# First weights in four loads and transposed by VectorE, in a gated convolution pair on one core

## The chip, the core and the metric

One NeuronCore of a Trainium2 chip. The time is the device time of one execution in microseconds (us). The engines are TensorE (PE), VectorE (DVE), ScalarE (ACT), GpSimd (POOL) and SyncE (SP); SP, ACT and POOL also issue DMAs, each on a queue of its own.

## The reference, cut to what matters

```python
def qconv_cg(x, w, theta):                 # 64 channels, the first 16 are the "base"
    yp = conv3x3(x[:, :16], w[:, :16])
    yr = conv3x3(x[:, 16:], w[:, 16:])
    d = sigmoid(2.0 * (yp - theta))
    return yp + d * yr

h = relu(bn(qconv_cg(x, w_a, theta_a), gamma_a, beta_a, mean_a, var_a))
h = bn(qconv_cg(h, w_b, theta_b), gamma_b, beta_b, mean_b, var_b)
return relu(x + h)                         # x: (16, 64, 56, 56), w: (64, 64, 3, 3), float32
```

## The kernel before

The 64 channels are four groups of 16. Each group has 32 partitions, since a partition holds one of two row parities of a channel, and each group of 32 rows of TensorE's array works alone, so four products with 32 rows run beside each other. Group 0 gives yp, groups 1 to 3 add up to yr. Values are split into a high and a low part (`x_hi`, `x_lo`, `w_hi`, `w_lo`), and three kinds of product are summed: high x with high w, high x with low w, low x with high w. With six taps (two slot offsets `c`, three columns `dx`) that makes 18 units for a visit of a group to a block: units 0 to 5 need `w_hi`, the second half of it from unit 3 on; units 6 to 11 need `w_lo`; units 12 to 17 need `x_lo`. TensorE's program is written out in steps, one unit of each active group for a step (L554). Group 2 begins its first visit at step 6 and group 3 at step 12; until then a product that nobody reads (L580) stands in their place. At step 24 a small transpose of the parameters stands (L572), from which VectorE works out the batch norms' constants. The first block takes 7 slots of the first image. In all there are 108 blocks, of the first and the second convolution in turn.

The start is what the change is about:

- SP loads all of `w_a` as it lies in memory, output channels on 64 partitions (L402, 144 KB), then chunks of x (L371), then `w_b` in four loads by group (L411, 36 KB each), input channels to be. ACT issues two of the x loads.
- VectorE writes zeros (L756 to L767), then copies w_a with the parities side by side into `w_pad` (L769, L771); ScalarE does two rows of it (L652).
- TensorE multiplies zeros from `h_lo`, which GpSimd has set (L437), two small products and seven large ones (L500), then does 12 transposes of `w_pad` into PSUM (L494), then one small product.
- ScalarE makes `w_hi` from PSUM (L640), VectorE the high part of the first x chunk (L839), `w_lo` (L776) and the `x_lo` parts (L835).
- GpSimd makes the identity matrix (L438, L440), issues ten loads of parameters (L445), then writes zeros into the padding of `h_hi` and `h_lo` and goes on to the weights of the edges.
- The second weights already go the other way: the four loads (L411), eight transposes by VectorE (L790), ScalarE's high part (L645), VectorE's low part (L797).

Engines run their own programs in order and meet at semaphores.

Of the kernel before, what the change touches and what calls it, by code (L numbers as in the profile page):

```python
# [5 lines left out]
ALU = mybir.AluOpType  # L6
# [4 lines left out]
P = 128  # L11
# [22 lines left out]
SMALL, WARM, BRIDGE = 2, 7, 1  # L34
# [6 lines left out]
def gated_conv_pair_kernel(nc, x, w_a, theta_a, gamma_a, beta_a, mean_a, var_a,  # L41
# [119 lines left out]
    with ExitStack() as ctx:  # L161
# [21 lines left out]
        NAT, PAD = C * TAPS * TAPS, (TAPS + 1) * TAPS * C * 2  # L183
        HALF_NAT = GR * TAPS * TAPS


        AT_B = NAT + PAD
        AT_T = AT_B + 5 * HALF_NAT
        early = sb("early", [P, AT_T + 2 * TAPS * P])
        w_nat_a = early[0:C, 0:NAT]  # L190

        w_pad = early[0:C, NAT:AT_B].rearrange("o (r b i q) -> o r b i q", r=TAPS + 1, b=TAPS, q=2)
        zeros_b = early[:, AT_B:AT_T].rearrange("p (z n) -> p z n", n=HALF_NAT)[:, 0:5:2]
        w_nat_b = early[:, AT_B:AT_T].rearrange("p (z n) -> p z n", n=HALF_NAT)[:, 1:5:2]

        w_t = early[:, AT_T:AT_T + 2 * TAPS * P].rearrange("p (t m) -> p t m", m=P)
        e_hi = sb("e_hi", [P, 2, EDGE_COLS], F32R)
        e_lo = sb("e_lo", [P, 2, EDGE_COLS], F32R)
        x_edge = early[:, 0:EDGE * W]
# [28 lines left out]
        wpad_ready = sem("wpad_ready")  # L228
        wpad_odd_ready = sem("wpad_odd_ready")
        wzeros_ready = sem("wzeros_ready")  # L230
        wbt_ready = sem("wbt_ready")
        zeros_ready = sem("zeros_ready")
        warm_done = sem("warm_done")
        wt_ready = sem("wt_ready")
# [107 lines left out]
        def natural_a(rows):  # L342

            return w_nat_a.rearrange("o (i a b) -> o a b i", a=TAPS, b=TAPS)[:, rows]
# [41 lines left out]
        def _(sp):  # L386
# [15 lines left out]
            sp.dma_start(w_nat_a, w_a.rearrange("o i a b -> o (i a b)")).then_inc(w_landed[0], 16)  # L402
# [16 lines left out]

            sp.wait_ge(wt_ready, 2)  # L420
# [14 lines left out]
        def _(pool):  # L435
            for lo, hi in ((0, P), (P, BANK)):
                nc.gpsimd.memset(h_lo[:, lo:hi].bitcast(F32), 0.0).then_inc(zeros_ready, 1)  # L437
# [9 lines left out]
            for n, t in enumerate((h_hi, h_lo)):  # L447
                if t is h_lo:
                    pool.wait_ge(zeros_ready, 2)
                    pool.wait_ge(warm_done, 1)  # L450
                nc.gpsimd.memset(t[:, 0:1].bitcast(F32), 0.0)
                nc.gpsimd.memset(t[:, 1::PITCH].bitcast(F32), 0.0).then_inc(hpads_zero, 2)
# [33 lines left out]
        def _(pe):  # L486
            def weights(c, bank):

                pe.wait_ge(wpad_ready, 3 + c)
                pe.wait_ge(wpad_odd_ready, 1 + c)  # L490
                for dx in range(TAPS):
                    to = psum[:, bank, dx * P:(dx + 1) * P].rearrange("p (c q) -> p q c", q=2)
                    for mq in range(2):
                        last = pe.transpose(to[:, mq], w_pad[:, 2 * c - mq + 1, dx].rearrange("o i q -> o (i q)"),  # L494
                                            ident[:])
                last.then_inc(wt_ready, 1)
# [72 lines left out]
            for step in sorted(steps):  # L569
                if step == 24:  # L570
                    pe.wait_ge(prmdup_ready, 2)
                    pe.transpose(psum[:, 7, 0:10], prm_dup[:].rearrange("n c q -> n (c q)"),  # L572
                                 ident[0:10, 0:10]).then_inc(prmT_ready, 1)
                for g in (2, 3):
                    if step < OFFSET[g]:

                        if step == 0:
                            pe.wait_ge(xhi0_ready, 1)
                            pe.wait_ge(whi_ready, 1)
                        pe.matmul(psum[:, g - 1, 0:SPARE], w_hi[0][g * ROWS:(g + 1) * ROWS, 0],  # L580
                                  x_hi[g * ROWS:(g + 1) * ROWS, 0, 1:1 + SPARE], start=True, stop=True)
                for g, visit, u in steps[step]:
                    b = visited(g, visit)
                    kind, n = blk = order[b]
                    if u == 0 and g == bank_groups(b)[0]:
                        if kind == "a":
                            if n == 0:
                                pe.wait_ge(xhi0_ready, 1)
                                pe.wait_ge(whi_ready, 1)
# [32 lines left out]
                    if g == 0 and u == 0 and b == 1:  # L622
                        pe.wait_ge(wlo_ready, 2)
                    if g == 0 and u == 0 and b == 2:
                        pe.wait_ge(rvar_ready, 1)
                    if u == 0 and b == WARM_BANK and g == bank_groups(b)[0]:
                        pe.wait_ge(warm_done, 1)
# [9 lines left out]
        def _(act):  # L637
            def weights_hi(c, bank):
                act.wait_ge(wt_ready, c + 1)
                nc.scalar.activation(w_hi[0][:, c * TAPS:(c + 1) * TAPS].rearrange("p t m -> p (t m)"),  # L640
# [330 lines left out]
```

## Time and profile before

| | us |
|---|---|
| runs | 436.45, 434.79, 434.56 |
| median | 434.79 |
| profiled execution, its own time | 434.86 |
| its span, first to last instruction | 433.0 |
| TensorE busy in the span | 425.9 |

The span is what the profile shows; the 1.9 us between it and the execution's own time lie around it.

### The profile page before, as it was taken

Reading aid. Unit: us, or ns where it says so; the run is one execution under the profiler, and the core shown is the slowest. Engines: PE = TensorE matmul, PEld = TensorE weight load, DVE = VectorE, ACT = ScalarE, POOL = GpSimd, SP = SyncE. Lnnn points to the kernel's source line nnn. Section 1 sums busy time; section 2 is a strip of 40 time slices with the busy share of each in tenths; the row PEclk is TensorE's granted clock in tenths of the full one; section 3 lists DMA queues with packets and bytes.
Section 4 is the critical chain, followed back from the end, with each engine's and each line's share of the span. In section 5 each row is a group of like instructions: output and inputs, shape, how many; then the busy total and the mean of one; then the engine's idle time right before and its main releaser. Section 6 shows DMA issues by size and latency. Waiting matters only on the chain.

```text
span 433.0 us, 17317 instructions
## 1 busy us (share of the span) xinstructions
PE 425.9 (98%) x7817; PEld 423.0 (98%) x7817; DVE 246.6 (57%) x420; ACT 198.8 (46%) x337; POOL 30.2 (7%) x83
## 2 busy tenths in 40 slices
PE   9999999999999999999999999999999999999994
PEld 7999999999999999999999999999999999999993
DVE  6767644753764663574375385366357367436535
ACT  5765444534544553453453453354345355434322
POOL 6041000000000100000000000011000000000001
PEclk9999999999999999999999999999999999999998
DMA  8435116241515110420624161161623322012044
GB/s 170 83 78 99 27 27 124 50 98 30 122 28 101 25 28 3 100 51 2 125 58 81 37 122 30 27 122 25 122 49 61 67 49 45 8 27 49 8 93 94
DMA packets 119802, 27.57 MB, mean 64 GB/s; under 512 B 119408, under 2 KB 119664, under 8 KB 119728
## 3 DMA queue, kind: packets, MB, share of 16 engines
q1 hardware_dynamic: 117296, 25.99, 29.4%
q8 instruction: 62, 1.02, 1.0%
q10 hardware_dynamic: 2112, 0.46, 0.5%
q14 instruction: 12, 0.10, 0.1%
q0 software_dynamic: 320, 0.00, 0.0%
HBM read 13.60 MB, written 12.85 MB: 61 GB/s over the span
## 4 chain that ended last, share of the span: by engine, by line
PE 97%; DVE 1%; issue 0%; ACT 0%; POOL 0%; DVEq 0%; POOLq 0%
PE acc L554 96%; PE acc L500 1%; DVE mix L858 0%; DVE rows_out L906 0%; PE acc L494 0%; PE acc L580 0%; ACT mix L697 0%; DVE rows_out L948 0%; DVE rows_out L903 0%; POOL h_lo L437 0%; ACT rows_out L719 0%; DVEq L857 0%; POOLq L960 0%
## 5 line engine op out<-in xcount | busy, mean ns | idle before, releaser
L554 PE MATMUL acc<-x_lo,w_hi 32*128 32x456 f32 (+1 forms) x1392 | 248.4, 358 | 0.0
L554 PE MATMUL acc<-x_hi,w_lo 32*128 32x456 f32 (+1 forms) x1392 | 248.2, 358 | 0.0
L554 PE MATMUL acc<-x_hi,w_hi 32*128 32x456 f32 (+1 forms) x1392 | 247.7, 358 | 0.0
L554 PE MATMUL acc<-h_hi,w_lo 32*128 32x512 f32 x1152 | 241.4, 390 | 0.0
L554 PE MATMUL acc<-h_lo,w_hi 32*128 32x512 f32 x1152 | 241.0, 390 | 0.0
L554 PE MATMUL acc<-h_hi,w_hi 32*128 32x512 f32 x1152 | 240.7, 389 | 0.0
L554 PEld LDWEIGHTS acc<-x_hi,w_hi 32*128 32x128 f32 x1392 | 208.5, 183 | 0.4
L554 PEld LDWEIGHTS acc<-x_hi,w_lo 32*128 32x128 f32 x1392 | 208.6, 183 | 0.2
L554 PEld LDWEIGHTS acc<-x_lo,w_hi 32*128 32x128 f32 x1392 | 208.5, 183 | 0.0
L554 PEld LDWEIGHTS acc<-h_hi,w_hi 32*128 32x128 f32 x1152 | 181.3, 183 | 0.1
L554 PEld LDWEIGHTS acc<-h_lo,w_hi 32*128 32x128 f32 x1152 | 181.3, 184 | 0.1
L554 PEld LDWEIGHTS acc<-h_hi,w_lo 32*128 32x128 f32 x1152 | 181.0, 184 | 0.2
L697 ACT ACTIVATE mix<-acc,gate_bias 128x448 f32<-128x448 f32 (+2 forms) x108 | 69.5, 644 | 176.4 <-PE acc L554 176.3
L858 DVE TENSOR_TENSOR mix<-mix,acc 128x448 f32<-128x448 f32 (+2 forms) x108 | 68.4, 634 | 105.2 <-PE acc L554 104.9
L885 DVE SCALAR_TENSOR_TENSOR rows_out<-acc,inv,x 128x504 f32<-128x504 f32 x46 | 34.0, 739 | 53.1 <-ACT mix L697 53.1
L719 ACT ACTIVATE rows_out<-rows_out,shift 128x504 f32<-128x504 f32 (+1 forms) x49 | 35.0, 715 | 33.5 <-DVE rows_out L906 32.8
L702 ACT ACTIVATE z<-acc,shift,inv 128x448 f32<-128x448 f32 (+1 forms) x58 | 40.8, 704 | 0.0
L893 DVE SCALAR_TENSOR_TENSOR mix<-mix,inv,z 128x448 f32<-128x448 f32 (+1 forms) x58 | 38.9, 671 | 2.0
L715 ACT ACTIVATE h_hi<-mix 128x448 fp32r<-128x448 f32 (+1 forms) x58 | 32.2, 564 | 13.8 <-DVE mix L893 13.4
L835 DVE TENSOR_TENSOR x_lo<-x,x_hi 128x448 fp32r<-128x448 f32 (+3 forms) x52 | 33.5, 678 | 7.1 <-ACT x_hi L665 7.0
L906 DVE SCALAR_TENSOR_TENSOR rows_out<-mix,inv,rows_out 128x504 f32<-128x504 f32 (+1 forms) x48 | 35.7, 744 | 1.7
L921 DVE SCALAR_TENSOR_TENSOR h_lo<-mix,h_hi 128x448 fp32r<-128x448 f32 (+2 forms) x64 | 33.1, 567 | 0.1
(85 smaller groups left out, 157.3 us busy)
## 6 DMA issues: line engine op xcount, KB each, us to landing
out_dram<-rows_out SPq DMA_DIRECT2D x95, 126.0 KB, 2.6
x<-in_x_dram SPq DMA_DIRECT2D x28, 392.0 KB, 5.3
early<-in_x_dram SPq DMA_DIRECT2D x4, 112.0 KB, 4.0
out_dram<-rows_out SPq DMA_DIRECT2D x3, 112.0 KB, 2.8
x<-in_x_dram SPq DMA_DIRECT2D x3, 98.0 KB, 3.8
x<-in_x_dram SPq DMA_DIRECT2D x1, 294.0 KB, 4.2
x<-in_x_dram SPq DMA_DIRECT2D x1, 280.0 KB, 4.9
x<-in_x_dram SPq DMA_DIRECT2D x1, 196.0 KB, 4.1
```

The lines of the kernel that those rows point to most:

```text
L500: return pe.matmul(psum[:, WARM_BANK, 0:n], h_lo[:, 0:P], h_lo[:, 0:n], start=True, stop=True)
L554: return pe.matmul(sums(bank, blk), w[g * ROWS:(g + 1) * ROWS, tap], moving(blk, part, c, dx, g), start=(u == 0 and (alone or g == bank_gr ...
L697: nc.scalar.activation(mix_rows(b), yp_rows(b), ACT.Sigmoid, scale=ALPHA, bias=gate_bias[:, k:k + 1]).then_inc(gate_ready, 1)
L702: nc.scalar.activation(z_of(n).rearrange("p (s w) -> p s w", w=W), yp_rows(b), ACT.Identity, scale=inv[:, 0:1], bias=shift[:, 0:1]).then_i ...
L715: nc.scalar.activation(in_middle(h_hi, n), as_block(mixed(b), n), ACT.Relu).then_inc(hhi_ready, 1)
L719: nc.scalar.activation(out_of(m), out_of(m), ACT.Relu, bias=shift[:, 1:2]).then_inc(out_ready, 1)
L835: nc.vector.tensor_tensor(split_chunk(x_lo, n), x_chunk(n), split_chunk(x_hi, n).bitcast(F32), ALU.subtract).then_inc(xlo_ready, 1)
L858: nc.vector.tensor_tensor(mix_rows(b), mix_rows(b), yr_rows(b), ALU.mult).then_inc(gated_ready, 1)
L885: nc.vector.scalar_tensor_tensor(to, yp_rows(b), inv[:, 1:2], was, ALU.mult, ALU.add).then_inc(zb_ready, 1)
L893: nc.vector.scalar_tensor_tensor(mixed(b), mixed(b), inv[:, 0:1], z_of(n), ALU.mult, ALU.add).then_inc(summed_ready, 1)
L906: nc.vector.scalar_tensor_tensor(out_of(m), mixed(b), inv[:, 1:2], out_of(m), ALU.mult, ALU.add).then_inc(summed_ready, 1)
L921: nc.vector.scalar_tensor_tensor(part[0], part[1], 0.0, part[2], ALU.max, ALU.subtract).then_inc(hlo_ready, 2 // images)
```

## The change

- `w_a` comes in four loads by group, of 36 KB each, in the form that `w_b` has: group 0 from SP, group 1 from ACT ahead of its x loads, groups 2 and 3 from GpSimd ahead of all its other work. They land in `natural`, beside columns of zeros that VectorE sets after the first x padding.
- VectorE does the transposes, eight by 32x32 blocks into `w_t` in SBUF. `w_pad`, its copies and TensorE's 12 transposes are gone.
- ScalarE makes the high part of the first x chunk, then `w_hi` of tap 0 alone (`wtap_ready`), then the rest of the first half, then the second half. The first unit waits for tap 0 only, unit 1 for the first half.
- VectorE makes both halves of `w_lo` from SBUF before its `x_lo` parts.
- TensorE's products on zeros read a constant in both operands, ten large and four small, one after the other up to the first unit; no wait ahead of them, and none for them afterwards.
- `w_b`'s loads wait until w_a is transposed, since they go to the same place. `x_edge` has its own space.

```diff
-SMALL, WARM, BRIDGE = 2, 7, 1
+WARM, BRIDGE = 10, 4
...
+        x_edge = sb("x_edge", [P, EDGE * W])
...
+        natural = sb("natural", [P, 5, HALF_NAT])
+
+        w_t = sb("w_t", [P, 2 * TAPS, P])
...
+        def load_w(eng, w, g, done):
+
+            eng.dma_start(natural[g * ROWS:(g + 1) * ROWS, 1:4:2],
+                          w.rearrange("(h o) (g i) a b -> g o h (i a b)", h=2, g=GROUPS)[g]).then_inc(done, 16)
...
-            sp.dma_start(w_nat_a, w_a.rearrange("o i a b -> o (i a b)")).then_inc(w_landed[0], 16)
+            load_w(sp, w_a, 0, w_landed[0])
...
+
+            sp.wait_ge(wt_ready[0], 2)
             for g in range(GROUPS):
-                sp.dma_start(w_nat_b[g * ROWS:(g + 1) * ROWS],
-                             w_b.rearrange("(h o) (g i) a b -> g o h (i a b)", h=2, g=GROUPS)[g]
-                             ).then_inc(w_landed[1], 16)
+                load_w(sp, w_b, g, w_landed[1])
...
-            for lo, hi in ((0, P), (P, BANK)):
-                nc.gpsimd.memset(h_lo[:, lo:hi].bitcast(F32), 0.0).then_inc(zeros_ready, 1)
+            for g in (2, 3):
+                load_w(pool, w_a, g, w_landed_pool)
...
+            def zeros(n):
+
+                return nc.const_aps.tensor(0.0, (P, n), F32).bitcast(F32R)
...
-                return pe.matmul(psum[:, WARM_BANK, 0:n], h_lo[:, 0:P], h_lo[:, 0:n], start=True, stop=True)
-
-            pe.wait_ge(zeros_ready, 1)
-            for n in range(SMALL):
-                zeros_product(P)
-            pe.wait_ge(zeros_ready, 2)
+                return pe.matmul(psum[:, WARM_BANK, 0:n], zeros(P), zeros(n), start=True, stop=True)
+
             for n in range(WARM):
                 zeros_product(BANK)
-            pe.wait_ge(ident_ready, 2)
-            for c in range(2):
-                weights(c, 6 + c)
             for n in range(BRIDGE):
-                mm = zeros_product(P)
-            mm.then_inc(warm_done, 1)
+                zeros_product(P)
...
-                                pe.wait_ge(whi_ready, 1)
+                                pe.wait_ge(wtap_ready, 1)
...
+                    if b == 0 and g == 1 and u == 1:
+                        pe.wait_ge(whi_ready, 1)
...
+            load_w(nc.scalar, w_a, 1, w_landed[0])
             act.wait_ge(xpads_zero, 1)
             load_x(nc.scalar, 0, 0, SHORT + 1, x_first[0], (1,))
             load_x(nc.scalar, 0, SHORT + 1, 2 * SHORT + 1, x_second, (1,))
-            weights_odd()
-            for c in range(2):
-                weights_hi(c, 6 + c)
             act.wait_ge(xcols_zero, 1)
+            act.wait_ge(x_first[0], 32)
+            nc.scalar.activation(split_chunk(x_hi, 0), x_chunk(0), ACT.Copy).then_inc(xhi0_ready, 1)
+
+            act.wait_ge(wt_ready[0], 1)
+            weights_hi(0, slice(0, 1)).then_inc(wtap_ready, 1)
+            weights_hi(0, slice(1, TAPS)).then_inc(whi_ready, 1)
+            act.wait_ge(wt_ready[0], 2)
+            weights_hi(0, slice(TAPS, 2 * TAPS)).then_inc(whi_ready, 1)
...
             zero_x_pads(0, 1)
+            nc.vector.memset(natural[:, 0:5:2], 0.0).then_inc(wzeros_ready, 1)
             zero_x_pads(1, X_IMGS)
...
+            def transposed(k, c):
+
+                for mq in range(2):
+                    for h in range(2):
+                        rows = filter_rows(natural[:, 2 * h:2 * h + 3].rearrange("p z n -> p (z n)"),
+                                           2 * c - mq + 1, slice(0, TAPS))
+                        to = w_t[:, c * TAPS:(c + 1) * TAPS].rearrange("p t (o q) -> p t o q", q=2)
+                        last = nc.vector.transpose(to[:, :, h * ROWS:(h + 1) * ROWS, mq],
+                                                   rows.rearrange("p i q b -> p b i q"))
+                last.then_inc(wt_ready[k], 1)
...
+            def first_weights():
+                dve.wait_ge(w_landed[0], 32)
+                dve.wait_ge(w_landed_pool, 32)
                 dve.wait_ge(wzeros_ready, 1)
                 for c in range(2):
+                    transposed(0, c)
+                for c in range(2):
+                    dve.wait_ge(whi_ready, c + 1)
+                    weights_lo(0, c)
...
-            dve.wait_ge(x_first[0], 32)
-            nc.vector.tensor_copy(split_chunk(x_hi, 0), x_chunk(0)).then_inc(xhi0_ready, 1)
-            for c in range(2):
-                weights_lo(c, 6 + c)
+            first_weights()
             for n in range(SOON):
                 split_lo(n)
```

## Rows read from the trace of the kernel before

**Rows 1.** The page: busy time, DMA queue, share of the chain by engine.
```profile
PE 425.9 (98%) x7817; PEld 423.0 (98%) x7817; DVE 246.6 (57%) x420; ACT 198.8 (46%) x337; POOL 30.2 (7%) x83
...
q0 software_dynamic: 320, 0.00, 0.0%
...
PE 97%; DVE 1%; issue 0%; ACT 0%; POOL 0%; DVEq 0%; POOLq 0%
```

**Rows 2.** The chain that ended last, in order of time: start, us, what.
```profile
0.99 3.78 PE acc L500 x9
4.78 1.22 PE acc L494 x12
...
6.28 0.55 PE acc L580 x2
...
8.83 414.39 PE acc L554 x6868
```

**Rows 3.** PE's timeline: start, us, instruction, count.
```profile
1.48 1.59 PE L500 MATMUL acc<-h_lo 128*128 128x512 f32 x3
...
2.01 1.48 PE L500 MATMUL acc<-h_lo 128*128 128x512 f32 x3
...
3.72 1.05 PE L500 MATMUL acc<-h_lo 128*128 128x512 f32 x2
...
7.15 0.36 PE L554 MATMUL acc<-x_hi,w_hi 32*128 32x398 f32 x2
...
8.79 0.37 PE L554 MATMUL acc<-x_lo,w_hi 32*128 32x398 f32 x2
...
10.98 0.17 PE L572 MATMUL acc<-ident,prm_dup 10*128 10x10 f32 x1
```

**Rows 4.** One stretch of PE: us, busy (instructions), granted clock, DMA share, GB/s.
```profile
2.50:5.00 2.50, 2.50 (x9) 1.00 0.99 212
```

**Rows 5.** VectorE's timeline, in brackets idle time before and its releaser.
```profile
0.83 0.62 DVE L756 MEMSET x<- 128x112 f32 x2 [0.83 <-PEq L960]
...
3.77 0.76 DVE L769 COPY early<-early 64x384 f32<-64x384 f32 x1 [1.02 <-DMA early<-in_L_conv_w_a_dram]
...
6.17 1.02 DVE L776 TENSOR_TENSOR w_lo<-acc,w_hi 128x384 fp32r<-128x384 f32 x2 [0.31 <-ACT w_hi L640]
...
9.58 0.29 DVE L846 COPY prm_dup<-prm_rows 10x64 f32<-10x64 f32 x2 [0.38 <-DMA prm_rows<-in_L_conv_var_b_dram]
...
17.87 1.92 DVE L790 STREAM_TRANSPOSE early<-early 128x96 f32<-128x96 f32 x8
```

**Rows 6.** ScalarE's timeline.
```profile
9.85 0.20 ACT L678 ACTIVATE probe<-probe 128x1 f32<-128x1 f32 x1
...
21.34 0.94 ACT L645 ACTIVATE w_hi<-early 128x384 fp32r<-128x384 f32 x2
```

**Rows 7.** DMA issues that touch 1.3 to 2.0: KB each, us to landing.
```profile
early<-in_L_conv_w_a_dram SPq DMA_DIRECT2D x1, 144.0 KB, 3.0
x<-in_x_dram ACTq DMA_DIRECT2D x1, 112.0 KB, 3.1
x<-in_x_dram SPq DMA_DIRECT2D x1, 98.0 KB, 3.9
```

**Rows 8.** The loads of w_b (L411): ns min/median/max, and landing.
```profile
L411 SPq DMA_DIRECT2D early<-in_L_conv_w_b_dram x4: 427/430/1691, 7.5 to 10.2; - x4
...
DMA to landing us min/median/max: 2.1/2.7/3.8
```

**Rows 9.** GpSimd's ten loads of parameters (L445), landing.
```profile
DMA to landing us min/median/max: 2.5/2.9/3.3
```

**Rows 10.** GpSimd's timeline.
```profile
0.73 0.56 POOL L437 MEMSET h_lo<- 128x128 f32 x2 [0.29 <-POOLq L960]
...
2.12 0.65 POOL L445 DMA_DIRECT2D prm_rows<-in_L_conv_theta_a_dram  x1 [0.28 <-issue]
...
4.20 0.49 POOL L445 DMA_DIRECT2D prm_rows<-in_L_conv_var_a_dram  x1
```

More of the change, by code:

```diff
@@ L227, in gated_conv_pair_kernel @@
         ident_ready = sem("ident_ready")
-        wpad_ready = sem("wpad_ready")
-        wpad_odd_ready = sem("wpad_odd_ready")
         wzeros_ready = sem("wzeros_ready")
[L231 to L234, printed above, removed]
+        wt_ready = [sem(f"wt_ready{c}") for c in "ab"]
+        w_landed_pool = sem("w_landed_pool")
+        wtap_ready = sem("wtap_ready")
         whi_ready = sem("whi_ready")
@@ L446, in _ @@
                                ).then_inc(prm_landed, 16)
[L447 to L450, printed above, removed]
+            for t in (h_hi, h_lo):
                 nc.gpsimd.memset(t[:, 0:1].bitcast(F32), 0.0)
@@ L570, in _ @@
                 if step == 24:
+                    pe.wait_ge(ident_ready, 2)
                     pe.wait_ge(prmdup_ready, 2)
@@ L588, in _ @@
                                 pe.wait_ge(xhi0_ready, 1)
-                                pe.wait_ge(whi_ready, 1)
+                                pe.wait_ge(wtap_ready, 1)
                             else:
@@ L637, in _, with weights_hi @@
         def _(act):
[L638 to L641 removed]
+            def weights_hi(k, taps):
+                return nc.scalar.activation(w_hi[k][:, taps], w_t[:, taps], ACT.Copy)
             def second_weights_hi(c):
[L644 to L652 removed]
+                act.wait_ge(wt_ready[1], 2)
+                weights_hi(1, slice(c * TAPS, (c + 1) * TAPS)).then_inc(whi_ready, 1)
             def split_hi(n):
@@ L764, in _ @@
             nc.vector.memset(probe[:], 0.0).then_inc(probe_zero, 1)
-            for q in range(2):
-                nc.vector.memset(w_pad[:, TAPS * q, :, :, q], 0.0).then_inc(wpad_ready, 1)
-            nc.vector.memset(zeros_b, 0.0).then_inc(wzeros_ready, 1)
-            dve.wait_ge(w_landed[0], 16)
-            nc.vector.tensor_copy(w_pad[:, 1], natural_a(slice(0, 2)).rearrange("o a b i -> o b i a")
-                                  ).then_inc(wpad_ready, 1)
-            nc.vector.tensor_copy(w_pad[:, 2:4, :, :, 0], natural_a(slice(1, 3))).then_inc(wpad_ready, 1)
@@ L773, in weights_lo @@
-            def weights_lo(c, bank):
-                dve.wait_ge(whi_ready, c + 1)
-                part = w_hi[0][:, c * TAPS:(c + 1) * TAPS].rearrange("p t m -> p (t m)")
-                nc.vector.tensor_tensor(w_lo[0][:, c * TAPS:(c + 1) * TAPS].rearrange("p t m -> p (t m)"),
-                                        psum[:, bank, 0:TAPS * P], part.bitcast(F32),
-                                        ALU.subtract).then_inc(wlo_ready, 1)
+            def transposed(k, c):
[7 more added lines that the diff above has]
+                last.then_inc(wt_ready[k], 1)
@@ new lines, in weights_lo @@
+            def weights_lo(k, c):
+                taps = slice(c * TAPS, (c + 1) * TAPS)
+                nc.vector.tensor_tensor(w_lo[k][:, taps], w_t[:, taps], w_hi[k][:, taps].bitcast(F32),
+                                        ALU.subtract).then_inc(wlo_ready, 1)
+            def first_weights():
+                dve.wait_ge(w_landed[0], 32)
+                dve.wait_ge(w_landed_pool, 32)
+                dve.wait_ge(wzeros_ready, 1)
+                for c in range(2):
+                    transposed(0, c)
+                for c in range(2):
+                    dve.wait_ge(whi_ready, c + 1)
+                    weights_lo(0, c)
@@ L780, in second_weights @@
             def second_weights():
                 dve.wait_ge(w_landed[1], 16 * GROUPS)
-                dve.wait_ge(wzeros_ready, 1)
                 for c in range(2):
-                    for mq in range(2):
-                        for h in range(2):
-                            at = AT_B + 2 * h * HALF_NAT
-                            rows = filter_rows(early[:, at:at + 3 * HALF_NAT], 2 * c - mq + 1, slice(0, TAPS))
-                            to = w_t[:, c * TAPS:(c + 1) * TAPS].rearrange("p t (o q) -> p t o q", q=2)
-                            last = nc.vector.transpose(to[:, :, h * ROWS:(h + 1) * ROWS, mq],
-                                                       rows.rearrange("p i q b -> p b i q"))
-                    last.then_inc(wbt_ready, 2)
+                    transposed(1, c)
@@ L794, in second_weights_lo @@
             def second_weights_lo(c):
                 dve.wait_ge(whi_ready, 3 + c)
-                taps = slice(c * TAPS, (c + 1) * TAPS)
-                nc.vector.tensor_tensor(w_lo[1][:, taps], w_t[:, taps], w_hi[1][:, taps].bitcast(F32),
-                                        ALU.subtract).then_inc(wlo_ready, 1)
+                weights_lo(1, c)
             chain = [0]
```

34 lines of the change are left out of this document (removed).

## The prediction, made before the changed kernel ran

> **What bounds the kernel now.** I read the page's totals first: TensorE (PE) is busy for 425.9 of 433.0 us and carries 97% of the chain that ended last [rows 1]. So nothing that another engine does is worth anything, unless it moves the moment at which PE's real work begins, stops PE later, or changes PE's speed. Second, the chain in order of time shows where that moment is [rows 2]: PE runs products on zeros from 0.99, the twelve transposes of the first weights from 4.78, and the first product on x at 6.28; the last row shown is 414.39 us of products from 8.83 in one piece, without a gap. The change touches nothing behind the second visit. The question is only whether the products after 6.28 come earlier or later.
>
> Third, the timeline of PE fixes the reference points [rows 3]. Four row groups share the array, so a "step" is four products; steps follow one another every 0.18 us: step 3, the first that needs the second half of w_hi, has its unit at 7.15, 0.87 after the first product at 6.28, and step 12, the first with x_lo, at 8.79, nine steps and 1.64 us later. The products on zeros start every 0.43 us (2.01 to 3.72 is four of them, 1.71 us) for 512 columns, so 1.2 GHz, the lower of the two levels. A step of 398 columns in 0.18 us is 2.4 GHz. The rise lies between 3.72 and 7.15; the granted-clock column shows 1.00 there too [rows 4], so it doesn't locate the rise, and I go by the spacing.
>
> **The change part by part.** Call W the moment at which all of w_a has landed.
>
> Before, W is 3.77 [rows 5], and behind it come VectorE's and ScalarE's copies, the transposes on PE, and w_hi from PSUM [rows 2, 5]: unit 3 is at W + 3.38.
>
> After, behind W: eight transposes on VectorE, of the same tile shape as those of the second weights, 1.92 us for eight [rows 5]; four are through after 3 x 0.24 + 0.32 = 1.04 (0.24 is 1.92 / 8, 0.32 is about the duration of one, since two overlap). Then ScalarE copies tap 0 alone, 128 elements: between a copy of one element, 0.20, and one of 384, 0.52 (two overlap in 0.94) [rows 6], I take 0.3. So the first unit can go at W + 1.04 + 0.03 + 0.3 + 0.03 = W + 1.4. The second half of w_hi needs all eight transposes and a 384-element copy: W + 1.92 + 0.03 + 0.52 + 0.03 = W + 2.50 for unit 3. Counted back by the 0.55 us of three steps, the start that matters is W + 1.95, and unit 3 decides, not unit 0. The later dependencies hold. The two subtractions for w_lo (0.51 each on VectorE, [rows 5]) end at W + 2.44 and about W + 3.0, and are wanted at steps 6 and 9, W + 3.05 and W + 3.6. The low part of the first x chunk ends at W + 3.6 and is wanted at step 12, W + 4.15. ScalarE's high part of the second chunk ends 0.5 after its weights, W + 3.0, wanted at step 6, W + 3.05: just in time. Break-even with before is thus W = 7.15 - 2.50 = 4.65.
>
> Now W itself. The four loads are 36 KB each. The SP and ScalarE ones start at about 0.74; SP's single 144 KB load took 3.0 us to land, and the same 36 KB form for w_b 2.1 to 3.8 [rows 7, 8]: they land at 3.8 or before, unless the x loads crowd them. The other two are issued by GpSimd, one after the other, and the second of these sets W. The trace shows GpSimd issuing only ten rows of 0.2 KB: 0.65 us for the first, 0.48 for another, 2.5 to 3.3 us from issue to landing [rows 9, 10]. GpSimd's body starts at 0.73, where the h_lo memset stands now; the second load is issued at 0.73 + 0.65 = 1.38. With the longest landing, 3.3, since a load of 36 KB must share the DMA engines with x, W = 4.7. In front of its first DMA GpSimd also stood idle for 0.28 without a releaser [rows 10]; if that is the price of a first DMA, W = 5.0. I take 4.8. Bounds: the shortest landing gives 1.38 + 2.5 = 3.9. Upwards, a row of prm is 32 packets (320 for ten, [rows 1]), and a weight load has 64 runs each way; if GpSimd's time grew with packets to four times 0.48, 1.9 us each, W = 0.73 + 0.28 + 1.9 + 1.9 + 2.4 (landing behind the end of the issue) = 7.2. I stay near the rows, because that end rests on a count of packets alone, and no row shows an issue of GpSimd's over 0.65.
>
> The Trainium skill ("DMA: Bandwidth & Descriptors", section on the anatomy of one DMA on the GpSimd path) says that many descriptors can be emitted before their cost shows, and fits 2.0 us plus bytes over 436 GB/s. By that, an estimate, a 36 KB load would land 2.1 us after its issue, W would be set by the other queues at about 3.8, and the early rival below would be the result. Even 0.2 KB took 2.5 to 3.3 here [rows 9], so I don't follow its figure.
>
> Moved with it: x's first chunk. ScalarE issues a weight load first (0.43, the shortest of w_b's, [rows 8]), so its x load starts near 1.2, and took 3.1 to land; SP's, behind the like issue, starts near 1.2 too and took 3.9 [rows 7]: x is there by 5.1. ScalarE now makes its high part (448 elements, at most 0.6), ending at 5.7; the weights are wanted from it at W + 1.07 = 5.9. So this is covered by the wait for W; were W early, each 0.1 us by which x is late would cost 0.1 at unit 0, and nothing at unit 3 until it is 0.9.
>
> PE's own queue: its zero products need no memset, so they start at about 0.82 instead of 0.99. A small one lies between 0.11 (a quarter of 0.43) and 0.25 (two took from 0.99 to 1.48, [rows 2, 3]); I take 0.15. Ten large and four small end their issue at 0.82 + 4.3 + 0.6 = 5.7. That is a floor: PE can't take the first real product before, 0.6 ahead of 6.28. With W = 4.8 the first unit is at 6.2, so PE idles some 0.5 us, less if the small ones are dear.
>
> Prm rows: GpSimd loses two memsets (0.56) and gains two loads (1.13), so the last row lands at 9.58 + 0.57 = 10.2, and its VectorE copies (0.29) end at 10.5; PE wants them at step 24, 10.98 before [rows 3, 5, 10]. Slack shrinks from 1.1 to about 0.6 with PE's own shift, and it is kept if the loads are dearer, because PE's start then moves by as much. VectorE's memsets, the reordered one of the zero columns too, end long ahead of W. w_b's loads wait for the first transposes, over at W + 1.95 = 6.75; they took 2.7 to land and are wanted at 17.87 [rows 5, 8], so even a queue at SP a few us long hides in that. x_edge on its own space removes a wait that had long been met.
>
> **Sum.** Unit 3 at 4.8 + 2.50 = 7.30 against 7.15: +0.15 us. The profiled execution took 434.86 us for its span of 433.0, and the median of the three runs is 434.79, so I forecast 435.0 us: no measurable change. One half percent is 2.2 us, about what a measurement of this kernel can tell from no change (its own three runs spread over 1.9). With the landing between 2.9 and 3.6 and the idle 0.28 counted or not, the likeliest case's own range is 434.5 to 435.6.
>
> **The rivals.**
> - Early: GpSimd's loads land in 2.5 us, W is 3.9, and PE's queue of zero products becomes the limit: -0.6 us, 434.3. For it: the early loads have little ahead of them. Against: x crowds the DMA engines from 2.5 to 5.0, at a share of 0.99 [rows 4]. Chance 0.13.
> - Slower by GpSimd's queue: its two issues cost more than 0.48 to 0.65. The place is W; the price is what both cost more, 1 to 1. It decides from 4.65 on, and passes 2.2 us only when W passes 6.9, so near its bound of 7.2 (+2.55, 437.4). One way to it is VectorE: its memsets run from 0.83 to about 2.3, beside the issues. The first prm row took 0.65, the one at 4.20, beside VectorE's copy of 3.77 to 4.53, 0.49 [rows 5, 10]; so I price this at 0.16 each, and 1.0 for both if they waited until 2.3. Chance 0.18, of which 0.04 is over 2.2 us; typical 436.0.
> - Slower by the clock: PE idles behind its zero products, then meets the first steps at 1.2 GHz. A step of 398 columns then takes 0.33 us, not 0.18, so each us at the lower level costs 0.45 us. In the trace the level had risen at most 6.2 us after PE's first product (0.99 to 7.15). If the idle stretch made it start afresh, 6.2 x 0.45 = 2.8 us, 437.8; half of that if it carries over in part, 436.4. For it: before has no such stretch between the last zero product and the first real one. Against: it is short beside 4.9 us of products. Chance 0.07, half of it over 2.2 us.
> - The forecast: chance 0.62.
>
> **Range and chances.** Range 434.2 to 436.4: it takes in the early rival and most of the GpSimd one, and leaves out what lies behind W = 6.2 and the worse half of the clock one. Faster by over 0.5% would need 2.2 us, and the floor of PE's queue allows 0.6: 0.01. Slower: 0.04 + 0.03, rounded up for what I may have missed: 0.07. Same: 0.92.
>
> **What would show it.** In the profile after: two GpSimd DMA issues of 0.5 to 0.7 from 0.73; VectorE's first transpose at 4.8, released by a GpSimd load; tap 0 on ScalarE at 5.9; the first product on x near 6.2, and unit 3 near 7.3; steps of 0.18 from there; the 10-element transpose near 11.1 with no idle ahead of it. The prediction is wrong if the first transpose starts after 6.8, if steps of 0.33 stand behind the first unit, or if PE idles ahead of the small transpose.

## The result

The changed kernel took 436.95 us (median of 22 runs, 436.27 to 437.51). The kernel before, run 22 times beside it, took 436.44 us, and not the 434.79 of its first three runs. The ratio is 1.0029, 95% interval 1.0019 to 1.004: 0.3% slower, less than the 0.5% that this work takes as a difference, but clear of noise. The forecast of 435.0, range 434.2 to 436.4, missed it. Five executions among all that follow took 468.79 to 1090.04 us (three of before, two of e9, its profiled one among them); they are disturbed, and no count of clusters holds them.

The medians hide that both kernels fall into two clusters. Of 21 runs of before, 7 took 434.5 to 434.8 and 14 took 436.4 to 437.0. Of 22 runs of after, 11 took 436.3 to 436.9 and 11 took 437.0 to 437.5; ten of the latter have a mean granted clock of 0.990 to 0.992, all others 0.994 or more. Lower cluster against lower cluster after lost 1.8 us (0.4%), upper against upper 0.6. There are thus two questions: what the 1.8 us are, and what makes the clusters.

The profile of after is of the lower cluster: its own time is 436.57 us, its span 434.7, against 434.86 and 433.0. Its page, totals and shares of the chain, beside [rows 1]:

```profile
PE 426.2 (98%) x7809; PEld 424.0 (98%) x7809; DVE 246.1 (57%) x423; ACT 197.9 (46%) x337; POOL 30.8 (7%) x83
...
PE 95%; POOL 1%; DVE 1%; DMA 1%; issue 1%; ACT 0%; POOLq 0%; DVEq 0%
```

TensorE is as busy as before (426.2 for 425.9). The extra time is not work but waiting, and GpSimd and a DMA have come into the chain. The chain in order of time, beside [rows 2]:

```profile
1.34 1.26 POOL natural L341 x2
...
3.46 4.34 POOL prm_rows L433 x9
7.80 4.18 DMA prm_rows<-in_L_conv_var_b_dram
...
12.00 0.30 DVE prm_dup L812 x2
...
12.43 0.20 PE acc L543
12.63 412.22 PE acc L524 x6826
```

What the end goes back to is no longer the first product on x, but the parameter rows that the small transpose of step 24 wants. It stands at 12.43 where [rows 3] have 10.98.

TensorE's timeline, beside [rows 3]:

```profile
0.78 5.19 PE L478 MATMUL acc<-const-float32-0.0 128*128 128x512 f32 x14 [0.78 <-PEq L926]
7.15 0.52 PE L551 MATMUL acc<-x_hi,w_hi 32*128 32x398 f32 x2 [1.18 <-ACT w_hi L609]
...
8.01 0.36 PE L524 MATMUL acc<-x_hi,w_hi 32*128 32x398 f32 x2
...
12.43 0.20 PE L543 MATMUL acc<-ident,prm_dup 10*128 10x10 f32 x1 [0.43 <-DVE prm_dup L812]
```

The first product on x is at 7.15, 0.87 later than at 6.28, behind 1.18 us of idle time. Unit 3 is at 8.01, 0.86 behind 7.15 before: the delay comes from the first product, not from unit 3. Without another wait step 24 would stand at 10.98 + 0.87 = 11.85. It stands 0.58 later. Behind the stall the products of that step start with it at 12.44 and the next ones 0.29 later, where steps otherwise follow after 0.18:

```profile
12.44 0.45 PE L524 MATMUL acc<-x_hi,w_hi 32*128 32x398 f32 x1
...
12.73 0.33 PE L524 MATMUL acc<-x_hi,w_hi 32*128 32x398 f32 x1
```

That is another 0.11, in all 0.87 + 0.58 + 0.11 = 1.56. ScalarE's fourth gate activation, the first one that waits for TensorE, is 1.57 later (21.86 for 20.29), and the span is 1.7 longer; the last 0.1 isn't located.

ScalarE's timeline of the start, and VectorE's, beside [rows 5, 6]:

```profile
4.94 1.28 ACT L634 ACT_TABLE_LOAD   x1 [4.94 <-DMA x<-in_x_dram]
6.23 0.58 ACT L634 ACTIVATE x_hi<-x 128x448 fp32r<-128x448 f32 x1
6.72 1.01 ACT L609 ACTIVATE w_hi<-w_t 128x128 fp32r<-128x128 f32 x3
```

```profile
5.20 1.86 DVE L741 STREAM_TRANSPOSE w_t<-natural 128x96 f32<-128x96 f32 x8 [2.84 <-issue]
7.35 1.03 DVE L747 TENSOR_TENSOR w_lo<-w_t,w_hi 128x384 fp32r<-128x384 f32 x2 [0.28 <-ACT w_hi L609]
...
12.00 0.29 DVE L812 COPY prm_dup<-prm_rows 10x64 f32<-10x64 f32 x2 [1.66 <-DMA prm_rows<-in_L_conv_var_b_dram]
```

x landed at 4.94. ScalarE then loads its table for 1.28 us, and only then makes the high part and tap 0. GpSimd's timeline, beside [rows 10]:

```profile
1.34 1.26 POOL L341 DMA_DIRECT2D natural<-in_L_conv_w_a_dram  x2 [0.89 <-POOLq L926]
...
3.46 0.52 POOL L433 DMA_DIRECT2D prm_rows<-in_L_conv_theta_a_dram  x1 [0.24 <-issue]
...
7.80 0.48 POOL L433 DMA_DIRECT2D prm_rows<-in_L_conv_var_b_dram  x1
```

Its first DMA starts at 1.34, not at 0.73. The landings (DMA issues that touch 1.3 to 2.0, and 2.0 to 2.7) are 2.3 us for the first weight load and 2.7 as the median of both, so 3.1 for the second: about 2.05 + 3.1 = 5.15, and VectorE goes at 5.20.

```profile
natural<-in_L_conv_w_a_dram POOLq DMA_DIRECT2D x1, 36.0 KB, 2.3
...
natural<-in_L_conv_w_a_dram POOLq DMA_DIRECT2D x2, 36.0 KB, 2.7
```

### The profile page after: what moved, and what is told of

Read it like the earlier page. It is cut to its first block, busy times and chain, and to the rows that moved or that the text cites. A ratio compares the mean times of both kernels' runs of the same rounds, so it can differ in the third digit from the quotient of the medians.

```text
span 434.7 us, 17302 instructions
## 1 busy us (share of the span) xinstructions
PE 426.2 (98%) x7809; PEld 424.0 (98%) x7809; DVE 246.1 (57%) x423; ACT 197.9 (46%) x337; POOL 30.8 (7%) x83
## 4 chain that ended last, share of the span: by engine, by line
PE 95%; POOL 1%; DVE 1%; DMA 1%; issue 1%; ACT 0%; POOLq 0%; DVEq 0%
PE acc L524 95%; POOL prm_rows L433 1%; DMA prm_rows<-in_L_conv_var_b_dram 1%; DVE mix L824 0%; DVE rows_out L872 0%; POOL natural L341 0%; ACT mix L664 0%; DVE rows_out L914 0%; DVE prm_dup L812 0%; DVE rows_out L869 0%; POOL ident L428 0%; PE acc L543 0%; POOL ident L426 0%; POOLq L428 0%; ACT rows_out L686 0%
## 5 line engine op out<-in xcount | busy, mean ns | idle before, releaser
L524 PE MATMUL acc<-x_lo,w_hi 32*128 32x456 f32 (+1 forms) x1392 | 252.2, 358 | 0.0
L524 PE MATMUL acc<-x_hi,w_lo 32*128 32x456 f32 (+1 forms) x1392 | 251.8, 358 | 0.0
L524 PE MATMUL acc<-x_hi,w_hi 32*128 32x456 f32 (+1 forms) x1392 | 251.6, 357 | 0.0
L524 PE MATMUL acc<-h_hi,w_lo 32*128 32x512 f32 x1152 | 245.0, 390 | 0.0
L524 PE MATMUL acc<-h_lo,w_hi 32*128 32x512 f32 x1152 | 244.5, 389 | 0.0
L524 PE MATMUL acc<-h_hi,w_hi 32*128 32x512 f32 x1152 | 244.4, 389 | 0.0
L524 PEld LDWEIGHTS acc<-x_lo,w_hi 32*128 32x128 f32 x1392 | 212.7, 183 | 0.0
L524 PEld LDWEIGHTS acc<-x_hi,w_hi 32*128 32x128 f32 x1392 | 212.5, 183 | 0.1
L524 PEld LDWEIGHTS acc<-x_hi,w_lo 32*128 32x128 f32 x1392 | 212.6, 183 | 0.0
L524 PEld LDWEIGHTS acc<-h_hi,w_hi 32*128 32x128 f32 x1152 | 184.4, 183 | 0.0
```

The source lines that it names most:

```text
L524: return pe.matmul(sums(bank, blk), w[g * ROWS:(g + 1) * ROWS, tap], moving(blk, part, c, dx, g), start=(u == 0 and (alone or g == bank_gr ...
```

## The experiments

Times are medians; "before" is the kernel before, timed beside each set. Clusters are given as counts, because a median between two clusters says little. The three waits are taken first, the clock second. Each kernel computes the whole function; e6 also transposes zeros that nobody reads.

| run | us | ratio to before, 95% | clusters |
|---|---|---|---|
| e1 before again | 434.87 | 0.9988 (0.997 to 1.0007) | 7 at 434.5 to 434.9, 5 at 436.4 to 436.8 |
| e2 table early | 436.58 | 1.0020 (1.0006 to 1.0033) | 12 at 436.5 to 436.9 |
| e3 no GpSimd loads | 437.28 | 1.0033 (1.0014 to 1.0053) | 3 at 435.6 to 435.7, 9 at 437.1 to 438.9 |
| e4 both | 434.79 | 0.9978 (0.9965 to 0.9992) | 12 at 434.6 to 435.0 |
| e5 fewer zeros | 434.87 | 0.9990 (0.9973 to 1.0008) | 9 at 434.6 to 435.0, 3 at 436.0 to 436.6 |
| e6 transposes instead | 434.72 | 0.9974 (0.9958 to 0.9990) | 12 at 434.6 to 435.0 |
| e7 rows by ScalarE | 437.67 | 1.0052 (1.0030 to 1.0075) | 2 at 436.0 to 436.4, 6 at 437.6 to 437.9, 1 at 439.1 |
| e8 high part on VectorE | 434.78 | 0.9979 (0.9963 to 0.9994) | 12 at 434.6 to 434.9 |
| e9 before with the constant | 434.88 | 0.9990 (0.9974 to 1.0007) | 9 at 434.5 to 435.0, 1 at 436.7 |
| e10 third chunk split | 434.53 | 0.9975 (0.9961 to 0.9990) | 12 at 434.1 to 434.9 |
| e11 rows by SP | 435.59 | 1.0008 (0.9992 to 1.0024) | 8 at 435.3 to 435.8, 4 at 436.7 to 436.9 |
| e12 before once more | 436.61 | | 1, upper |
| e13 split, shorter zeros | 434.50 | 0.9990 (0.9974 to 1.0006) | 9 at 434.3 to 435.0, 3 at 435.8 to 436.4 |
| e14 after, longer zeros | 436.45 | 1.0026 (1.0012 to 1.0040) | 12 at 436.2 to 436.7 |

**e1, the kernel before again.** No edit.

> The kernel before, unchanged, against itself. Its 22 times lie in two clusters, 434.5 to 434.8 and 436.4 to 437.0 us. If the clusters come from TensorE's clock rising at a different moment of the start, a run of the upper cluster shows steps of 0.33 us instead of 0.18 behind the first product at 6.28, about 4 us of them (1.9 / 0.45). If they come from a wait, the steps stay at 0.18 and a gap of 1.9 us stands somewhere. Ratio 1.000 either way.

The two clusters came back, 7 to 5. In the five sets in which before was timed, 76 of its runs lie at 435.5 or below and 62 at 435.8 to 437.0. Its profile was of the lower cluster, so it didn't decide; e12's does. e1's profile shows a mean granted clock of 0.945 at 434.82 us, a usual time, which no run explains, so the mean clock alone doesn't tell a run's cluster.

**e2, the table load ahead of the wait.**

```diff
+            act.wait_ge(probe_zero, 1)
+            nc.scalar.activation(probe[:, 2:3], probe[:, 3:4], ACT.Copy)
             act.wait_ge(xcols_zero, 1)
             act.wait_ge(x_first[0], 32)
```

> The kernel after, with one activation of a single element ahead of ScalarE's wait for x, so that the table load of 1.28 us no longer hangs on that wait. Theory (the parameter rows at step 24 decide, the late first product is covered by them): the first product moves from 7.15 to about 6.65, step 24 stays at 12.4, the span stays at 434.7. Rival (the late first product is the loss): the span falls by the same 0.5 us to 434.2.

The lower cluster gained nothing: 436.58, span 434.6. The chain still goes through the rows, with the small transpose at 12.32 (12.43 in after):

```profile
7.80 4.06 DMA prm_rows<-in_L_conv_var_b_dram
...
12.32 0.20 PE acc L543
12.52 412.21 PE acc L524 x6817
```

So the late first product was covered by the late rows. The start of TensorE's products shows what the table load had hidden:

```profile
6.79 0.53 PE L551 MATMUL acc<-x_hi,w_hi 32*128 32x398 f32 x2 [0.92 <-ACT w_hi L609]
...
7.48 0.35 PE L524 MATMUL acc<-x_hi,w_hi 32*128 32x398 f32 x2
...
7.80 0.45 PE L524 MATMUL acc<-x_hi,w_hi 32*128 32x398 f32 x2
```

The first product is at 6.79 for 7.15, and unit 3 at 7.80 stands 0.32 behind unit 2, not 0.18: here unit 3 waits for the second half of w_hi, as the prediction had it. Its VectorE began to transpose at 5.32, and 5.32 + 2.50 = 7.82. In after the second half of w_hi would have let unit 3 go at about 7.76, so of the 0.86 by which it is late there some 0.6 is W and 0.25 the table load.

Something was gained in the upper cluster: none of e2's 12 runs is above 436.9, where after has 11 of 22 at 437.0 or more. TensorE stands idle for 0.92 us here, for 1.18 in after. One of e2's runs has a mean clock of 0.991 all the same, at 436.56.

Why the table load waits in after is read from the traces and not from the compiled program: with two waits ahead of the first activation it began with the landing of x (4.94); in before, with one wait there, it ran at 2.45, ahead of the landing at 3.77 that its activation waited for. So it seems that of two waits one is hung on the table load.

**e3, w_a's loads by SP and ScalarE alone,** the table load as in after.

```diff
             load_w(sp, w_a, 0, w_landed[0])
+            load_w(sp, w_a, 2, w_landed[0])
...
-            for g in (2, 3):
-                load_w(pool, w_a, g, w_landed_pool)
...
             load_w(nc.scalar, w_a, 1, w_landed[0])
+            load_w(nc.scalar, w_a, 3, w_landed[0])
```

> The kernel after, with w_a's groups 2 and 3 issued by SP and ScalarE instead of GpSimd, the table load still behind the wait for x. Theory (parameter rows decide): the last parameter row lands near 9.3 instead of 11.98, no stall at step 24; the first product is at 7.3 to 7.5, since x is issued 0.4 us later and the table load still follows it; step 24 at 12.1, span 434.2 to 434.5. Rival (what decides is W, the landing of w_a behind GpSimd): W falls from 5.2 to about 3.5 and the first product with it, by 1.0 us or more, span 433.5.

Three runs lie at 435.6 to 435.7, 0.8 below after's lower cluster. The other nine are above 437.0. The profile is one of those. The rows were there by 10.26. W fell to 3.36, yet the first product stayed at 7.16, held by the table load, so the rival fell. TensorE's stretches (length, busy and count, granted clock, DMA share, GB/s) show something new:

```profile
0.00:4.50 4.50, 3.72 (x9) 3.04 (x10) 2.48 (x14) 0.00 (x0) 3.46 (x12) 1.00 0.44 95
4.50:7.90 3.40, 1.67 (x21) 1.50 (x23) 1.26 (x6) 2.95 (x6) 3.25 (x10) 1.00 1.13 223
7.90:11.30 3.40, 3.40 (x48) 3.40 (x44) 2.64 (x8) 2.58 (x5) 0.00 (x0) 0.51 1.20 202
11.30:14.70 3.40, 3.40 (x82) 3.40 (x79) 0.72 (x5) 0.47 (x2) 0.00 (x0) 0.99 0.97 199
```

The products on zeros end early, TensorE idles 1.74 us, and then, although it works without a pause from 7.16 on, the granted clock is 0.51 from 7.9 to 11.3, the level of 1.2 GHz. 48 products fit there, 82 into the next stretch of the same length. That is the clock rival of the prediction. Six of the nine have the mean clock that one such fall gives, 0.990 to 0.992; the two longest, 438.5 and 438.9, have 0.996, and what made them longer stays open.

**e4, both edits.**

> Both edits: loads of w_a by SP and ScalarE, table load ahead of the wait for x. Theory (two waits in a row, neither worth anything alone): x's high part ends at 5.8, tap 0 at 6.2, first product 6.25, unit 3 near 7.1, no stall at step 24, span 433.0 or like before. Rival (the transposes on VectorE are slow in themselves, or TensorE's idle stretch costs clock): the span stays at 434 or above although both waits are gone.

434.79, in one narrow cluster, 1.8 below after and level with before's lower cluster. First product at 6.12, no stall at step 24. The two edits give back the whole of the lower cluster's loss: the table alone gives 0 (e2), the loads alone 0.8 (e3), both 1.8. TensorE still stands idle for 0.64 us ahead of its first product on x here, and no run lies in an upper cluster. Its chain now begins with x:

```profile
1.68 3.43 DMA x<-in_x_dram
...
5.20 0.58 ACT x_hi L635
5.78 0.21 ACT w_hi L607
...
6.12 0.53 PE acc L549 x2
```

**e7 and e11, GpSimd's loads by themselves.** To price W without the rows, five of the ten rows go to another queue, the table load is early, GpSimd keeps its weight loads.

```diff
-            for n, v in enumerate(rows):
+            for n, v in enumerate(rows[:5]):
...
+            for n, v in enumerate([theta_b, gamma_b, beta_b, mean_b, var_b]):
+                nc.scalar.dma_start(...)   # e7, behind its x loads; e11: sp.dma_start, behind image 0
```

> The kernel after with the table load early (as e2) and five of the ten parameter rows issued by ScalarE behind its x loads; GpSimd keeps its two loads of w_a. It isolates the loads by GpSimd: W stays at 5.2, the rows are there by 10. Theory (in after the parameter rows are worth the stall of 0.6 at step 24 and all that follows it, W is worth about 0.6 by itself): unit 3 at W + 2.5 = 7.7, no stall, span 433.5, time 435.3. Rival (W alone gives the loss): 434.6 span as in e2.

e7 missed its aim. ScalarE's five issues pushed its table load to 5.41, the first product came at 7.72, and the forecast of 435.3 was wrong by 0.7 to 1.1 even in its lower cluster.

```profile
5.41 1.28 ACT L637 ACT_TABLE_LOAD   x1 [5.41 <-issue]
6.71 0.20 ACT L637 ACTIVATE probe<-probe 128x1 f32<-128x1 f32 x1
6.81 0.56 ACT L640 ACTIVATE x_hi<-x 128x448 fp32r<-128x448 f32 x1
```

It does show that without the wait for rows a late first product costs its own length: it is 1.44 late, and the span, 434.4, is 1.4 above before's.

> The kernel after with the table load early and five of the ten parameter rows issued by SP behind the loads of the first image; GpSimd keeps its two loads of w_a and ScalarE has no more to issue than in after. W stays at 5.2. Theory (W by itself costs about 0.6): first product at 6.7, unit 3 at W + 2.5 = 7.7, rows there by 10, span 433.5, time 435.4. Rival (W hurts less than that): 433.0.

e11 puts the rows on SP. The first product is at 6.73 and eight runs lie at 435.3 to 435.8 (forecast 435.4), so W at 5.2 costs 0.7 by itself against e4, and the rows on GpSimd cost another 1.1 against e2. Four runs are at 436.7 to 436.9; the profile, with a clock of 0.51 from 7.0 to 10.4 behind 1.73 us of idling, is one of them. Two of the four have a mean clock of 0.991 like it, the other two 0.994, so these may have another cause.

**e12, before once more.** No edit.

> The kernel before once more, one profile. If it falls into the upper cluster (one in two), the theory of the clock says: the products on zeros run at 0.43 us, and behind the first product on x steps of 0.33 us stand for some 4 us. If it falls into the lower, it is the profile of before again.

It fell into the upper cluster, 436.61, span 434.8. Its timeline of TensorE against [rows 2, 3]:

```profile
0.99 3.78 PE L500 MATMUL acc<-h_lo 128*128 128x128 f32 x9 [0.99 <-POOL h_lo L437]
4.70 1.54 PE L494 MATMUL acc<-ident,early 64*128 64x64 f32 x12
6.17 0.47 PE L500 MATMUL acc<-h_lo 128*128 128x128 f32 x1
...
6.58 0.70 PE L554 MATMUL acc<-x_hi,w_hi 32*128 32x398 f32 x2
...
7.08 0.53 PE L554 MATMUL acc<-x_hi,w_hi 32*128 32x398 f32 x2
...
7.41 0.53 PE L554 MATMUL acc<-x_hi,w_hi 32*128 32x398 f32 x2
...
10.49 0.34 PE L554 MATMUL acc<-x_lo,w_hi 32*128 32x398 f32 x1
```

The same instructions up to 4.7, the same start. But the steps are 0.33 apart (7.08, 7.41) until 10.06, and step 12 is at 10.49 for 8.79: 1.70 of the 1.8 us. In before's own profile the steps are of 0.18 from 6.97 on, so the clock rose over 3 us later here, with no idle stretch ahead of it. One profile of each cluster shows this; that all upper runs of before are like it is inferred from their equal times.

**e5 and e6, what holds the clock.** Both are e4 with nine large products on zeros, ending at 4.7; e6 puts twelve transposes of zeros behind them.

```diff
-WARM, BRIDGE = 10, 4
+WARM, BRIDGE = 9, 0
...
+            pe.wait_ge(ident_ready, 2)      # e6 only
+            for n in range(12):
+                pe.transpose(psum[:, WARM_BANK, 0:C], nc.const_aps.tensor(0.0, (C, P), F32), ident[:])
```

> The kernel of e4 with nine large products on zeros and no small ones, so that TensorE works from 0.78 to about 4.7 and then stands idle until the first product on x at 6.1. Theory (the upper cluster of before, 1.9 us above the lower, comes from the clock, which counts the products on zeros up to the first real one): besides runs at 434.8 there are runs at 436 or more, with steps of 0.33 us in their start. Rival (the products on zeros beyond 4.7 us do nothing): one cluster at 434.8 as in e4.

> The kernel of e5 with twelve transposes of zeros of the size that before has, in the place of before's, 4.7 to 5.8; their result is read by nobody. It differs from e4 only in what TensorE does between 4.7 and 5.8: transposes instead of products. If transposes hold the clock like products, one cluster at 434.8 as in e4. If they count as idle time, the clusters of before and of e5 come back, some runs at 436 or more. That would explain before's upper cluster.

With TensorE idle for 1.0 us (e5), 3 of 12 runs are at 436.0 to 436.6; with ten and four products (e4) or with transposes (e6), none. That points to the later products on zeros holding the clock, though 3 of 12 against none is weak, and e5's profile is of its lower cluster, so that a late clock in the other three isn't seen. I found no sign that transposes are what spoils it. The Trainium skill ("TensorE: Matmul & The Clock Gate", Part 4 on transposes) says that transposes don't count as busy in the same way, and that the higher clock doesn't engage for them. By it e6 should look like e5; 0 of 12 against 3 of 12 speaks against that here, but too weakly to settle it.

**e9, before with the constant.** One part of the change alone: nine large products from 0.78, no wait, then before's transposes.

```diff
-SMALL, WARM, BRIDGE = 2, 7, 1
+SMALL, WARM, BRIDGE = 0, 9, 1
...
-                return pe.matmul(psum[:, WARM_BANK, 0:n], h_lo[:, 0:P], h_lo[:, 0:n], start=True, stop=True)
+                return pe.matmul(psum[:, WARM_BANK, 0:n], zeros(P), zeros(n), start=True, stop=True)
```

> The kernel before with one part of the change alone: its products on zeros read the constant, wait for nothing and are nine large ones from 0.78 to 4.7 (then its own transposes, and one small product). e6 has the same row of products and twelve transposes behind them and has one cluster. Theory (the start of TensorE's work at 0.99 with small products and a wait in it is what lets the clock rise late in half of before's runs): one cluster at 434.8. Rival (the transposes with their waits are the cause): two clusters, 434.7 and 436.7, half and half.

One of ten runs in the upper cluster, against 10 of 29 for the kernel before beside it and 62 of 138 in all. No profile shows its usual start. It leans to the theory, that the earlier and unbroken row of products lets the clock rise in time, but ten runs don't prove it.

**e14, after with longer zeros.**

```diff
-WARM, BRIDGE = 10, 4
+WARM, BRIDGE = 13, 4
```

> The kernel after, with thirteen large and four small products on zeros, so that TensorE works up to its first product on x at 7.15 instead of standing idle for 1.2 us. Theory (the runs of after at 437.0 to 437.5, with a mean granted clock of 0.991, are those in which the clock falls once behind the idle stretch, and the stall at step 24 hides a part of it): one cluster, 436.3 to 436.9, no run with a clock of 0.991. Rival (the second cluster has another cause): it stays.

One cluster, 436.2 to 436.7, and no run below 0.993 in clock, where after had 11 of 22 at 437.0 or more. So the 1.2 us of idling are what after's upper cluster hangs on. That the clock falls there is inferred, since no profile is of that cluster: e3 and e11 show such a fall, and 3.4 us at half the clock take 0.004 off the mean, 0.991 for 0.995.

```profile
0.78 6.37 PE L478 MATMUL acc<-const-float32-0.0 128*128 128x512 f32 x17 [0.78 <-PEq L926]
7.32 0.53 PE L551 MATMUL acc<-x_hi,w_hi 32*128 32x398 f32 x2 [0.17 <-ACT w_hi L609]
```

The first product was 0.17 later here than in after, and the time didn't rise: again the rows cover it.

**e8, e10 and e13, a version beyond both.** e8 is e4 with the first chunk's high part on VectorE; e10 gives the third chunk its own load; e13 shortens the zeros of e10 to nine and two.

```diff
+                dve.wait_ge(x_first[0], 32)                  # e8, behind the eight transposes
+                nc.vector.tensor_copy(split_chunk(x_hi, 0), x_chunk(0)).then_inc(xhi0_ready, 1)
...
-            load_x(sp, 0, 2 * SHORT + 1, XS, x_landed[0])
+            load_x(sp, 0, 2 * SHORT + 1, 3 * SHORT + 1, x_third)      # e10
+            load_x(sp, 0, 3 * SHORT + 1, XS, x_landed[0])
```

> The kernel of e4 with the high part of the first x chunk made by VectorE again, so that ScalarE makes w_hi while x is still under way. x is there at 5.15, the cast takes 0.47, the first product goes at 5.65 to 5.7 instead of 6.12, if the products on zeros (ending their issue near 5.4) don't hold it: 0.4 us faster than e4, 434.35. If the queue of zeros is the floor at 5.7 or more, or w_lo comes late behind the cast, it is 434.5 to 434.8.

> The kernel of e8, with the load of the last 14 rows of slots of the first image split in two, so that the third chunk has a load and a semaphore of its own. e8 starts its products on x 0.45 earlier than e4 and ends no earlier; ScalarE makes the third chunk's high part at 7.92, behind its landing. Theory (the third chunk of x is the next wait): it lands near 6.9, no gap at step 12, the gain of e8 shows: span 432.4, time 434.35. Rival (DMA bandwidth is full, or a later wait takes the gain): third chunk no earlier than 7.6, span 432.8.

> The kernel of e10 with nine large and two small products on zeros instead of ten and four. In e10's profile the products on zeros ran at the lower clock until 6.06 and the first product on x went right behind them, although x's high part was done at 5.6. Theory (TensorE's own queue of zeros was the floor there): first product at 5.65 in every run, time 434.3 with less spread. Rival (a shorter row of zeros lets the clock rise late or fall): some runs at 435.5 or more, as in e5.

e8's first product came at 5.68, 0.44 earlier than e4's, and the end didn't move (434.78): the third chunk's high part waited for its load until 7.92. In e10 it is made at 6.93, and the median is 434.53, the lowest but for e13's 434.50. About half of the expected 0.4 is there. In its profile the products on zeros, still at 1.2 GHz, ran until the first product on x at 6.06: they are the floor in that execution (in e8's, with the higher clock sooner, the same row was over at 5.03). e13 takes that floor away, and nine runs lie at 434.3 to 435.0, but three are at 435.8 to 436.4. Its profile, 436.40, is one of them: x's high part lets the first product go at 5.90 only, behind 0.63 us of idling, and the steps are of 0.33 from 6.4 on. So the same row of zeros costs up to 0.4 us when it is long and 2 us in a quarter of the runs when it is short. e10 is the version to keep: 0.25% below before (0.9975), and 0.5% below after by its median (434.53 / 436.95, from different sets). Most of the first figure is freedom from the upper cluster: against before's lower cluster in the same set, median 434.81, e10 gains 0.3 us.

## Why the prediction was wrong

**The bound, and where to look.** Right. TensorE is busy for the same time, nothing behind the second visit moved, and everything came out of the first 12.6 us.

**The base.** Wrong. The forecast stood on the median of three runs, 434.79, two of them from before's lower cluster; the third, 436.45, was read as spread. Before's median over 22 runs was 436.44. The text allowed the clock to be late in the changed kernel only, although 62 of before's 138 runs lie in the upper cluster, and the one that was profiled has it late (e12). But the base isn't all: from lower cluster to lower cluster the forecast was +0.15, and the runs show +1.8. The two steps that failed are the next one and the parameter rows.

**"x is there by 5.1 ... its high part ..., ending at 5.7."** x was there at 4.94. The step that failed is what follows: ScalarE's first activation brings a table load of 1.28 us, a term that the sum doesn't have, and it began only when x had landed. The high part ended at 6.8, tap 0 near 7.1. The text said that unit 3 decides; unit 0 did, by 0.25. With the load out of the way unit 3 did decide (e2). The load alone cost nothing in after's lower cluster (e2) and 0.9 where the rows are in time (e3's lower cluster against e4). The three steps from the first product to unit 3 were counted at 0.55, though they took 0.87 in before as the same text says; it didn't change which wait decides.

**W.** Mis-sized: 4.8 forecast, 5.2 measured. The issues took 0.63 each and the second landing 3.1, as expected (0.65 and 0.48; 3.3), but GpSimd's first DMA started at 1.34 instead of 0.73. The idle time of 0.28 in [rows 10] was the sign; at the very start it was 0.89. The mechanism, that the second GpSimd load sets W and W sets unit 3, was right: e11 puts its price at 0.7 for W = 5.2. The bound of 7.2 by a count of packets never came near: GpSimd's queue moved 384 packets for 320, so 32 for each weight load, as many as for a row and not 64 each way.

**The transposes.** Right: 1.86 for 1.92. The second half of w_hi would have let unit 3 go at about 7.76, against 5.20 + 2.50 = 7.70.

**The parameter rows.** This is the second step that failed, and the one with the largest price: 1.1 us between e2 and e11's lower cluster. The text had the last row at 10.2 with a slack of 0.6, "kept if the loads are dearer, because PE's start then moves by as much". It landed at 11.98: GpSimd issued it 1.22 later than before, not 0.57 (0.61 of late start), and it took 4.2 us to land, not 3.0, though no landing of a row in [rows 9] was over 3.3. TensorE's start moved by 0.87 only. So instead of a slack of 0.6 there is a stall of 0.58, and everything ahead of it, up to 0.6 of late first product, was free. Why the landing took 1.2 us longer isn't settled. The DMA engines were busier in the 2 us behind the issue, at a share of 1.24 against 0.88 in before, and the loads of w_b began just ahead of it (7.75), where in before they began 0.96 behind it; no run separates these.

**The rivals.** The GpSimd queue rival named the right place with a chance of 0.18, but priced it by W alone. The clock rival (0.07) was right in kind and, as far as e14 shows, happened in half of after's runs. It cost 0.7 there rather than 2.8. A fall of 3.4 us as in e3 would cost 1.5 at 0.45 each, and the stall can hide some 0.6 of it. The floor of TensorE's zeros was seen for e10, at 6.06 instead of 5.7. The verdict by 0.5%, no difference, held, in part by luck: two thirds of before's runs beside it lay in the upper cluster, and from lower to lower cluster the loss was 0.4%.

## What to carry to other kernels

When an edit moves several things ahead of one start, list every wait of the consumer in order of time and put the new date beside each: here the first product, unit 3, step 24 and, in e8, the third chunk of x hid one another by less than a microsecond each, so that the early table load showed nothing in the lower cluster until the rows came in time too. Where a table load is due, see in the trace whether it starts only when the activation's input has landed; one element's activation ahead of that wait takes it off the path. And before forecasting from few runs, see whether the kernel has one time or two. What TensorE does ahead of its first real product turned two clusters into one here: e4, e6, e8, e10 and e14 have one cluster each in 12 runs, and their profiles show at most 0.66 us of idling there. Idle time isn't all of it, though: before has none and still has 62 of 138 runs in its upper cluster, and e13, with 0.63 us of idling and three products on zeros fewer than e10, has 3 of 12. What decides between these wasn't found.

## What the runs showed of the hardware

- The same instructions with the same start can meet TensorE's clock at either level: before's profile has steps of 0.18 us from 7.0 on, e12's has steps of 0.33 until 10.06.
- The clock can fall after TensorE has begun to work again: in e3 at 7.9, 0.7 us behind the first product on x, for 3.4 us.
- A DMA issued as GpSimd's first instruction of the kernel's body began 0.61 us later than a memset in the same place (1.34 against 0.73); the same row of 0.2 KB landed in 3.0 us in before and in 4.2 us in after.
- The first table load of ScalarE took 1.28 us wherever it stood (at 2.45 in before, 4.94 in after, 3.34 in e4), and in after the activation followed 0.01 us behind its end.
- The granted clock shown for a stretch at the start is 1.00 even while products of 512 columns are 0.43 us apart, so at the start the spacing has to be read.
